# The residual of an image added by one transfer of two rows a channel, in place of one transfer for each half

## The reference

```
wq = _quantize(weight, Wp, Wn)                  # ternary: Wp, 0 or -Wn
out = conv_general_dilated(_gn(x), wq, padding=((1, 1), (1, 1))) + bias
x = x + out                                     # the residual
```

## Time and profile before

| | |
|---|---|
| time, median of 3 runs | 567.81 us (567.1 to 568.34) |
| the profiled execution | 566.37 us, of which the traced span is 564.7 us |
| busy share of the span | PE 94%, DVE 96%, ACT 89%, POOL 28% |
| DMA queue q1 (hardware: SP's loads and stores) | 102.77 MB, 47.8% of the time of the 16 DMA engines |
| DMA queue q0 (software: POOL's residuals) | 49.78 MB, 45.6% |
| granted clock of PE | 0.996 |

### The profile page before, as it was taken

The page is one execution under the profiler, slowest core; times in us unless marked ns, Lnnn a source line. Parts: engine busy times, 40 slices in busy tenths (PEclk is TensorE's granted clock), DMA queues, the critical chain, the costliest instruction groups (busy, mean ns, idle before and its releaser), DMA issues.

```text
span 564.7 us, 9357 instructions
## 1 busy us (share of the span) xinstructions
PE 531.6 (94%) x3233; PEld 319.4 (57%) x3233; DVE 543.3 (96%) x506; ACT 504.0 (89%) x485; POOL 160.8 (28%) x106
## 2 busy tenths in 40 slices
PE   1898999999999999999999999999999999999995
PEld 0654555555555555555555555555555555555552
DVE  4998999999999999999999999999999999999994
ACT  4898999999999999999999999999999999999850
POOL 2020333311333321233332133333113333212330
PEclk9999999999999999999999999999999999999998
DMA  8539799999999999999999999999999999997767
GB/s 282 215 115 249 242 290 285 268 268 284 318 240 364 277 274 276 289 263 335 303 296 267 289 287 310 297 293 297 268 292 269 288 295 315 283 270 189 161 189 276
DMA packets 28104, 153.43 MB, mean 272 GB/s; under 512 B 3504, under 2 KB 3504, under 8 KB 28080
## 3 DMA queue, kind: packets, MB, share of 16 engines
q1 hardware_dynamic: 18576, 102.77, 47.8%
q0 software_dynamic: 8928, 49.78, 45.6%
q10 hardware_dynamic: 576, 0.59, 0.3%
HBM read 101.75 MB, written 51.38 MB: 271 GB/s over the span
## 4 chain that ended last, share of the span: by engine, by line
DVE 69%; issue 23%; PE 2%; ACT 2%; DMA 1%; DVEq 1%; ACTq 0%
DVE parts L607 26%; DVE y L622 18%; DVE plane L561 10%; DVE plane L567 9%; DVE newton L596 2%; PE odd_rows L766 1%; DMA x<-in_x_dram 1%; DVE plane L573 1%; DVEq L157 1%; PE even_rows L766 1%; DVE neg_var L585 1%; ACT junk L434 1%; DVE rstd L591 0%; ACT junk L402 0%; DVE parts L613 0%
## 5 line engine op out<-in xcount | busy, mean ns | idle before, releaser
L766 PE MATMUL odd_rows<-parts,w_lhsT 128*128 128x385 f16 (+1 forms) x1536 | 266.1, 330 | 7.8 <-DVE parts L607 7.5
L766 PE MATMUL even_rows<-parts,w_lhsT 128*128 128x385 f16 (+1 forms) x1536 | 265.6, 330 | 3.6 <-ACT c_sb L373 2.3
L607 DVE SCALAR_TENSOR_TENSOR parts<-plane,norm_scale,parts 128x1568 f16<-128x1568 f32 x127 | 233.6, 1844 | 1.7 <-ACT parts L388 1.7
L326 POOL TENSOR_TENSOR plane<-x 128x1512 f32<-128x1512 f32 x31 | 105.7, 3411 | 379.2 <-DVE parts L607 379.2
L766 PEld LDWEIGHTS even_rows<-parts,w_lhsT 128*128 128x128 f16 x1536 | 149.3, 98 | 109.9 <-issue 4.9
L388 ACT ACTIVATE parts<-plane,norm_scale 128x1568 f16<-128x1568 f32 x127 | 199.9, 1597 | 11.8 <-ACT plane L428 5.2
L766 PEld LDWEIGHTS odd_rows<-parts,w_lhsT 128*128 128x128 f16 x1536 | 147.9, 99 | 107.3 <-DVE parts L607 9.8
L434 ACT ACTIVATE junk<-x,negmean 128x3136 f16<-128x3136 f32 x32 | 92.9, 2903 | 0.1
L394 ACT ACTIVATE junk<-x 128x3136 f16<-128x3136 f32 x31 | 86.9, 2804 | 0.0
L622 DVE SCALAR_TENSOR_TENSOR y<-even_rows,out_scale,d_sb 128x784 f32<-128x784 f32 x62 | 63.7, 1027 | 0.0
L622 DVE SCALAR_TENSOR_TENSOR y<-odd_rows,out_scale,c_sb 128x784 f32<-128x784 f32 x62 | 63.6, 1026 | 0.0
(11 more groups left out here) (65 smaller groups left out, 110.1 us busy)
## 6 DMA issues: line engine op xcount, KB each, us to landing
x<-in_x_dram SPq DMA_DIRECT2D x64, 784.0 KB, 10.9
out_dram<-y SPq DMA_DIRECT2D x63, 784.0 KB, 5.7
y<-in_x_dram POOLq DMA_DIRECT2D x62, 784.0 KB, 11.9
out_dram<-y SPq DMA_DIRECT2D x2, 392.0 KB, 5.4
y<-in_L_conv_weight_dram ACTq DMA_DIRECT2D x1, 576.0 KB, 6.6
wp_sb<-in_L_conv_Wp_dram ACTq DMA_DIRECT2D x1, 0.5 KB, 7.5
wn_sb<-in_L_conv_Wn_dram ACTq DMA_DIRECT2D x1, 0.5 KB, 8.0
bias_sb<-in_L_conv_bias_dram ACTq DMA_DIRECT2D x1, 0.5 KB, 7.7
```

What stands on the lines that cost most here:

```text
L326: nc.gpsimd.tensor_tensor(plane[B][:, 0:PAIRS - 1, :], even[:, 0:PAIRS - 1, :], even[:, 1:, :], ALU.subtract).then_inc(plane_ready[B], 1)
L607: nc.vector.scalar_tensor_tensor(part(img, j, LO), plane[j][:], norm_scale[:, b_slice(img)], part(img, j, HI), ALU.mult, ALU.subtract).the ...
L766: ins = nc.tensor.matmul(product_ps(odd, b, b + 1)[:, 0, :, to:to + n], w_lhsT[:, prod, kw, :], part(img, prod, which)[:, b * BANK_ROWS:(b ...
```

## The change

`add_residual` is called once for an image instead of once for each half. It issues one DMA over all 56 rows, written as two rows of 1568 values a channel, so 1568 KB. It waits for the last of the four `output_rows` of the image, where the transfer of half 0 waited for the first two only. There is one semaphore `residual_added` for a buffer, and both stores wait for it.

```diff
-        residual_added = [[sem(f"residual_added{b}_{h}") for h in range(HALVES)] for b in range(X_BUFS)]
+        residual_added = [sem(f"residual_added{b}") for b in range(X_BUFS)]
...
                 def store(img, h):
-                    sp.wait_ge(residual_added[img.buf][h], residuals(img))
+                    sp.wait_ge(residual_added[img.buf], residuals(img))
                     sp.dma_start(in_dram(out_dram, img, h), half_of(y_sb[img.buf], h)).then_inc(y_stored[img.buf][h], 16)
...
-                def add_residual(img, h):
-
-                    written = img.half(h, 1, 1)
+                def add_residual(img):
+
+                    written = img.half(1, 1, 1)
                     if not isinstance(written, int):
                         written = pool.to_reg(written)
                     pool.wait_ge(consts_ready, 2 + len(TURNS))
                     pool.wait_ge(even_done, written)
                     pool.wait_ge(odd_done, written)
-                    y = y_sb[img.buf][:, 2 * ROWS * h:2 * ROWS * (h + 1), :].rearrange("p h w -> p (h w)")
-                    of = (out_dram if p else x_dram)[img.count(plus=-p * N_IMG)][:, h * 2 * COLS:(h + 1) * 2 * COLS]
-                    pool.dma_start(y, of, accum_op=ALU.add).then_inc(residual_added[img.buf][h], 16)
+                    y = y_sb[img.buf][:].rearrange("p (a h) w -> p a (h w)", a=HALVES)
+                    of = (out_dram if p else x_dram)[img.count(plus=-p * N_IMG)].rearrange("p (a c) -> p a c", a=HALVES)
+                    pool.dma_start(y, of, accum_op=ALU.add, max_dma_last_dim=8 * COLS).then_inc(residual_added[img.buf], 16)
...
                     if now and nxt:
-                        add_residual(now, 0)
-                        add_residual(now, 1)
+                        add_residual(now)
```

## The result

The changed kernel takes **570.03 us** (median of 17 runs, 568.42 to 571.9) against 567.32 us for the kernel before in the same runs (17 runs). The ratio is **1.0046, 95% interval 1.0033 to 1.0059**: 2.6 us slower. It was run once more beside other kernels: 569.53 against 567.02, ratio 1.0051 (1.0037 to 1.0065).

The account below looks back on a forecast made before the run. The prediction took DVE to bound the loop and a chain of DMA work the end. Later issue, generation and joint wait summed to +2.1 us on 567.81: 569.9 us, range 567.7 to 572.2 for 8 in 10.

Parts of the forecast that it names:

- What bounds the loop, and the cover of the transfers: In the loop: DVE, busy 16.55 of 16.62 us a slot, sets the pace; loads have 20 us of slack.
- The end as a chain of DMA work: Last 25 us: image 30's residual, its two stores, then image 31's stores end the kernel.
- The later issue, +0.25: At the end, the residual waits for DVE's last output rows, done at 543.71, where POOL had begun at 543.47: +0.25 us.
- The generation, +0.45: POOL generating twice the rows in one DMA: +0.45 us, the middle between 0 and 0.9.
- The landing at 555.4: Image 30's residual: last byte at 554.0, landing 1.4 us later at 555.4, instead of 554.7 before.
- The gap: No bytes between image 30's residual and its stores, 554.0 to 556.2, including 0.8 us from issue to first byte: 1.4 us cost.
- The end of the bytes at 564.05: The last stores, 3.21 MB at 410 GB/s from 556.2, end at 564.05 instead of 561.9: +2.1 us in all.
- fixed price of 3.3 us: Rival, whole transfer: each has a fixed price and one of two is saved, sum -1.65 us, 566.2; chance 0.07.
- the loop isn't bound by its DMAs: Answers a rival: the loop becomes bound by the DMA engines, 591 us at 3 us of gap; chance 0.08.
- the wider pattern: Rival, residual transfer: two rows a channel move a fifth slower, 9.4 us instead of 7.5, time 571.8; chance 0.05.
- The rule of the Trainium skill: Transfers to disjoint partition halves serialize, so prefer one; with its fixed 2.0 us a transfer, the sum is about no change.
- The signs named: DVE busy 16.55 us a slot, store pairs 0.35 us apart, empty windows around 555, last wait (L288) near 565.9, not 563.8.

Follow-up runs that it names:

- tail_two: The changed kernel, but with image 30's residual added by two transfers again, each with its store: 566.38 us, ratio 0.9997 to the kernel before.
- tail_one: The kernel before, but with only image 30's residual merged into one transfer, both its stores waiting for it: 570.47 us, ratio 1.0068.
- late_two: The kernel before, two transfers with a store each, but both transfers wait for the image's last output rows: 567.90 us, ratio 1.0028.
- joint_wait: The kernel before, still two transfers an image, but each store waits for both of them: 568.08 us, ratio 1.0025.
- tail_four: The kernel before, but with image 30's residual in four transfers, each with a store of its own: 568.59 us, ratio 1.0034.
- late_joint: The kernel before, two transfers an image, both issued after the last output rows, each store waiting for both: 570.22 us, ratio 1.0063.

## Why the prediction was right

The mechanism is the one forecast: an end that is a chain of DMA work, in which the joint wait opens a gap. That the number came so close is partly luck. The forecast of 569.9 us meets 570.03, but it was counted from 567.81, where the kernel before had 567.32 in the same runs. As differences, 2.1 us were forecast and 2.5 to 2.7 came, and within the 2.1 some terms were too small and one too large.

*Point by point, against the second profile of the changed kernel, whose DVE is level with that of before.*

- **What bounds the loop, and the cover of the transfers**: right, shown by the windows and by tail_two, though the cover shrank from some 20 us to about 13.
- **The end as a chain of DMA work**: right, shown by tail_one and tail_two, which move the whole cost with one transfer.
- **The later issue, +0.25**: mis-sized. Between the start of POOL's issue and DVE's last row there were -0.24 us before and are 0.57 now: 0.81. I had counted when DVE ends, not POOL's waking from a wait that before never held it. Alone (late_two), with POOL waking 1.25 us late, it cost 1.0 to 1.6.
- **The generation, +0.45**: 1.20 us against 0.86, +0.34, between the two ends (the sign named was 0.9 or 1.7): partly fixed, partly by rows.
- **The landing at 555.4**: at 555.5. That is two errors that cancel. The two terms above sum to 1.15, not 0.70, and the residual's bytes do end 0.5 us later than forecast, at 554.5. But the landing follows 0.9 us behind them, not 1.4. The 1.4 of before had been read in a window (553 to 554, 299 GB/s) in which the residual's last packets and the first store's are mixed.
- **The gap**: predicted from 554.0 to 556.2, seen from 554.5 to 556.2, with the 0.8 us from a store's issue (555.5) to its first byte as assumed. The small gaps of before did vanish: the windows from 557 to 564 stand at 386 to 433 GB/s, where before 341 and 320 were among them. (Outside these gaps the stores of before ran at 388 to 439, not at the 401 to 414 that the prediction read.) Alone, joint_wait cost 1.4 us, the size in the sum.
- **The end of the bytes at 564.05**: 564.2. The sum of 2.1 us against 2.6 (2.7 and 2.5 between the medians): what is missing comes after the last full window, where the last wait ended 1.9 us later before (561.9 to 563.8) and ends 2.3 us later now (564.2 to 566.5). I had no term for the packets that trail. The other 0.2 is the end of the bytes.
- **The rivals**: no fixed price of 3.3 us is saved (tail_four, late_joint); the loop isn't bound by its DMAs (tail_two, and DVE's 16.55 us in each slot); the wider pattern isn't slower (201 to 232 GB/s, and the same data packets). The rule of the Trainium skill that spoke for the change ("DMA: Bandwidth & Descriptors", Rules for kernel authors) is about transfers to two halves of the partitions. Here each half has all 128 partitions, and the two do run one after the other, as it says, but joining them saved nothing.
- **The signs named**: the gap near 555, the store pairs together and DVE's 16.55 us were seen. L288, said near 565.9, was seen at 566.5 and, in the first profile, 567.5.

## What to carry to other kernels

Two transfers in a queue that feed two consumers are a pipeline: here merging them saved nothing that could be told, and let the DMA engines stand empty for landing plus issue where nothing else was queued. In a loop bound by an engine that is hidden; look at the last iteration, where it is not, and keep the transfers apart at least there. A wait that now really waits costs more than the lateness of what it waits for: POOL started 0.57 to 1.25 us after DVE's last row.

## What the runs showed of the hardware

- A DMA that accumulates onto SBUF moved 201 to 232 GB/s in the windows that it filled, plain stores 386 to 439.
- A store on SP's queue, issued at 550.48 in the kernel before, moved no bytes that can be told while the residual on POOL's queue was going on: the windows from 550 stand at 215, 213 and 232 GB/s, the residual's rate, and rise to 299 only from 553.
- POOL wrote the descriptors of 128 rows of 6272 bytes in 0.86 us and of twice as many in 1.20.
- SP's issue of a store took 0.33 us before, but 2.32 us in the first profile of the changed kernel (L246), with two stores of image 30 issued 1 us earlier and unfinished; the DMA engines were full meanwhile, so no cost shows. In late_joint a hold of 2.1 us came just before they ran short of work. That a full queue holds the issue was not tried.
- A GpSimd addition over two SBUF tensors held up DVE's two-tensor instructions for 6.4 us.
